# A fused convolution block on one Trainium2 core: the last group of its state stage in halves over three bank pairs, later weights on GpSimd, the triangle stage's input normalised group by group, convolutions issued in tap rows

## What is computed

```python
def _gn(v, G=32, eps=1e-05):
    m, s = mean and var over axes (1, 2, 4)
    return (g - m) / jnp.sqrt(s + eps)
x = x + L0(_gn(x))   # window attention
x = x + L1(_gn(x))   # state layer
x = x + L2(_gn(x))   # triangle product
x = x + L3(_gn(x))   # recurrence over 28 rows
```

```python
x1 = silu(depthwise_conv3x3(grouped_1x1(x, w1)))
u, z = in_proj(x1);  u = silu(conv1d_3taps(u) + conv1d_b)
dt, B, C = x_proj(u);  delta = softplus(dt @ dt_proj + b)
h = exp(delta * A) * h + (delta * u) * B      # scan over 784 pixels, per state n
y = sum over n of h_n * C_n;  y = (y + u * D_param) * silu(z)
x1 = out_proj(y);  x1 = (x1 - mu) * rsqrt(var + 1e-5) * gamma + beta
return grouped_1x1(x1 * silu(grouped_1x1(x, w2)), wout)
```

## Time and profile before

| | us |
|---|---|
| median of 3 runs | 523.81 |
| lowest, highest | 522.98, 526.88 |
| the profiled execution | 523.52 |
| its span, first to last instruction | 521.7 |
| mean granted TensorE clock | 0.862 of full |

### The profile page before, as it was taken

The page is one execution under the profiler, slowest core; times in us unless marked ns, Lnnn a source line. Parts: engine busy times, 40 slices in busy tenths (PEclk is TensorE's granted clock), DMA queues, the critical chain, the costliest instruction groups (busy, mean ns, idle before and its releaser), DMA issues.

```text
span 521.7 us, 10477 instructions
## 1 busy us (share of the span) xinstructions
PE 365.1 (70%) x3722; PEld 242.5 (46%) x3722; DVE 385.2 (74%) x687; ACT 304.9 (58%) x571; POOL 224.7 (43%) x201
## 2 busy tenths in 40 slices
PE   4189988887989788669857356144594354988885
PEld 3057666665755332323312112021574224977874
DVE  3897898898883698986999599995547595644444
ACT  4247888878775998893797424023865602434333
POOL 3626866774652519857869526750250000000000
PEclk9999999999899997986879667565796585999999
DMA  5110000000404031040000000000000000111111
GB/s 134 9 12 3 3 0 0 0 1 0 106 3 108 0 69 38 1 107 0 0 1 1 0 0 0 0 0 1 2 1 5 0 1 0 19 19 20 22 22 22
DMA packets 23879, 9.52 MB, mean 18 GB/s; under 512 B 20521, under 2 KB 22313, under 8 KB 23849
## 3 DMA queue, kind: packets, MB, share of 16 engines
q1 hardware_dynamic: 23720, 9.13, 8.8%
q0 software_dynamic: 128, 0.01, 0.1%
HBM read 2.00 MB, written 1.61 MB: 7 GB/s over the span
## 4 chain that ended last, share of the span: by engine, by line
DVE 29%; PE 26%; ACT 19%; issue 15%; SPq 5%; POOL 4%; DMA 1%; DVEq 1%; POOLq 0%; ACTq 0%
PE pair L1435 4%; DVE pair L1698 4%; DVE Hs L1705 3%; PE pair L993 3%; SPq L317 3%; PE pair L1130 3%; DVE Ts L1599 2%; PE pair L1198 2%; PE pair L1046 2%; ACT PT L647 2%; PE pair L1114 2%; POOL Pr L451 2%; DVE hC L1718 2%; ACT gates L943 2%; POOL pp L591 1%
## 5 line engine op out<-in xcount | busy, mean ns | idle before, releaser
L451 POOL TENSOR_TENSOR Pr<-Pr,rc 128x392 f32<-128x392 f32 x64 | 54.3, 880 | 41.3 <-DVE rc L1615 41.3
L485 POOL TENSOR_TENSOR YA<-YA,hC 128x784 f32<-128x784 f32 x28 | 52.8, 1886 | 38.0 <-DVE hC L1718 36.4
L1198 PE MATMUL pair<-BCf,sel 96*128 96x392 bf16 x128 | 38.5, 405 | 33.1 <-DVE Hs L1705 26.2
L1705 DVE TENSOR_TENSOR_SCAN Hs<-dA,pair 128x784 f32<-128x784 f32 x32 | 57.2, 1786 | 1.1
L1593 DVE TENSOR_REDUCE mx<-pair 128x8 f32<-128x392 f32 x64 | 32.9, 555 | 14.6 <-PE pair L993 14.6
L1198 PEld LDWEIGHTS pair<-BCf,sel 96*128 96x128 bf16 x128 | 10.7, 106 | 69.2 <-issue 67.0
L647 ACT ACTIVATE PT<-pair 128x512 f32<-128x512 f32 x64 | 37.7, 592 | 7.9 <-PE pair L1035 7.6
L1035 PE MATMUL pair<-ident,Pr 128*128 128x128 f32 x256 | 37.8, 287 | 2.4 <-ACT PT L647 1.2
L1718 DVE TENSOR_TENSOR hC<-Hs,pair 128x784 f32<-128x784 f32 x28 | 26.6, 950 | 14.5 <-PE pair L1198 14.5
L769 ACT ACTIVATE dA<-DL,Aneg 128x784 f32<-128x784 f32 x32 | 29.1, 941 | 13.5 <-DVE Hs L1705 13.4
L653 ACT ACTIVATE Pr<-Ts 128x392 f32<-128x392 f32 x64 | 34.5, 541 | 3.1 <-DVE Ts L1599 2.6
(11 more groups left out here) (216 smaller groups left out, 943.9 us busy)
## 6 DMA issues: line engine op xcount, KB each, us to landing
SX<-XP SPq DMA_DIRECT2D x48, 112.2 KB, 2.3
XT<-in_x SPq DMA_DIRECT2D x4, 392.0 KB, 5.4
out<-Os SPq DMA_DIRECT2D x28, 56.0 KB, 1.8
NB<-in_L_conv_x_proj_w SPq DMA_DIRECT2D x4, 3.0 KB
DW<-in_L_conv_dw SPq DMA_DIRECT2D x4, 1.1 KB
vec<-in_L_conv_b_qkv POOLq DMA_DIRECT2D x3, 0.5 KB, 6.0
W<-in_L_conv_w_qkv SPq DMA_DIRECT2D x1, 48.0 KB
BL<-in_L_conv_bi SPq DMA_DIRECT2D x3, 0.5 KB
```

Source lines behind the costliest of these rows:

```text
L451: eng.tensor_tensor(pg, pg, bcast(rc[:, g, :], 2, WT), ALU.mult).then_inc(pn_r, 1)
L485: eng.tensor_tensor(y, y, hC[:, n % NHC, :], ALU.add).then_inc(g_ya, 1)
L1198: ins = eng.matmul(SPREAD[s][:, HT * h:HT * h + HT], sel[:, n, :], upper(BCf[:, c % 2, s, HT * h:HT * h + HT]), start=True, stop=True)
L1705: eng.tensor_tensor_scan(Hs[:, n % 2, :], dA[:, n % NA, :], SPREAD[0], 0.0, ALU.mult, ALU.add).then_inc(v_s, 1)
```

## The change

- **Bank pairs.** `x2` of group 3 and `out`, `var` of group 2 move from pair 3 to pair 2. The last group's `out`, `var`, `wout` have pairs 2, 3 and 1 (`TAIL`), each bank with its own half.
- **Order in the slots.** `times_b(c+1, 0)` and its spread now come before the last `times_c` of group c. Convolutions are issued in pieces of one or two rows of taps between the spreads. In group 1 `out(0)`, `var(0)`, `gate(2)`, `x2(2)`, `inner(3, ·)` change places; in group 2 `x2(3)` comes before the spread of slot 7 and `gate(3)` behind all spreads. ScalarE's list in group 1 is reordered: `copy_bc(2, xC)` earlier, Ln and Exp paired, `decays(2, ·)` behind all the silus.
- **Gamma and beta.** Gamma goes into ScalarE's copy `cS`; beta and the gate become one VectorE instruction, `norm`, in place of `shift` on VectorE and `gated` on GpSimd.
- **Group 3.** VectorE also does `residual(1)`, `residual(2)`, the statistics of groups 0 and 1, and `norm(2)` between its slots, and `times_c(6)` before scan 7. GpSimd does `later_weights`, `later_biases`, the zeroing (only the pads of `XR`) and the skip term between its sums.
- **The tail**, for the last group, goes in halves of 392 columns. `spare` issues bf16 matmuls of 512 columns whose result nobody reads: 8, 6, 3, 3, 3, 4, 4 of them. ScalarE normalises groups 0 to 2 for the triangle stage itself (`Identity` with scale and bias) while the last group is still on its way; the last group's statistics go through Sqrt on ScalarE and a reciprocal on VectorE.
- **Memory.** `XR` becomes `XR0`, which lies over `SX`, and `XR1`.

```diff
+        TAIL = dict(out=2, var=3, wout=1)
+        def tail_result(name, h):
+            return pairs[TAIL[name]][:, h, 0:HT]
...
+        LAST_GROUP = {("x2", 3): 2, ("out", 2): 2, ("var", 2): 2}
...
+            def skip_term():
+                eng.wait_ge(a_ud, 1)
+                eng.wait_ge(v_c, DS * (J - 1) + 1)
+                y = YA[:, (J - 1) % 2, :]
+                eng.tensor_tensor(y, y, S1[:, 0, 0:T], ALU.add).then_inc(g_ud, 1)
+            def pads():
+                eng.wait_ge(p_["conv"], 2 * J)
+                eng.memset(XR0[:, :, :, W:32], 0.0).then_inc(t_zz, 1)
+                eng.wait_ge(v_dl, J)
+                eng.memset(XR1[:, :, :, H:32], 0.0).then_inc(t_zz, 1)
...
+            def later_weights():
+                loaded(eng, 2)
+                eng.tensor_scalar(vec[:, V_BO:V_BO + 1], vec[:, V_BO:V_BO + 1], 0.5, None, ALU.mult).then_inc(g_w, 1)
+                eng.tensor_scalar(W4[:, U_M:U_M + 4, :], W4[:, U_M:U_M + 4, :], 0.5, None, ALU.mult).then_inc(g_w, 1)
+                eng.wait_ge(g_w, 2)
+                eng.tensor_tensor(BD[:, U_A:U_Z, :].rearrange("p u (g c) -> p u g c", g=G), bcast(W4[:, U_A:U_Z, :], 2, G),
+                                  bcast(bcast(bd[:, :], 1, U_Z - U_A), 3, C), ALU.mult).then_inc(g_w, 1)
...
+                    pads()
+                    later_weights()
+                    skip_term()
+                    eng.wait_ge(g_ud, 1)
+                    add(3, 1)
+                    later_biases()
+                    add(3, 2)
+                    add(3, 3)
+                    scaled(2)
+                    eng.wait_ge(p_["z"], J)
+                    eng.wait_ge(p_["u"], 2 * J)
+                    eng.memset(Zc[:], 0.0).then_inc(t_zz, 1)
+                    add(3, 4)
+                    add(3, 5)
+                    add(3, 6)
...
                     decays(1, 5)
-                    sp_l(2)
                     out_m(0)
-                    sp_w(2)
                     copy_bc(2, 1, "xC")
                     decays(1, 6)
+                    sp_l(2)
+                    var_ln(0)
+                    sp_w(2)
+                    var_exp(0)
+                    decays(1, 7)
                     silu_conv(3, 0)
+                    silu_z(2)
                     silu_conv(3, 1)
-                    var_ln(0)
-                    decays(1, 7)
-                    var_exp(0)
...
+                    eng.activation(S1[:, 0, 0:T], US[:, J - 1, :], ACT.Identity, scale=vec[:, V_D:V_D + 1]).then_inc(a_ud, 1)
                     decays(3, 4, 5)
                     out_m(2)
-                    decays(3, 6, 7)
+                    decays(3, 6)
                     var_ln(2)
                     var_exp(2)
...
+            for h in range(2):
+                eng.wait_ge(p_["out"], J + h)
+                eng.activation(sq[:, columns(h)], tail_result("out", h), ACT.Square).then_inc(c_["out"], 1)
+                eng.activation(cS[:, columns(h)], tail_result("out", h), ACT.Identity, scale=vec[:, V_GA:V_GA + 1])
+            for h in range(2):
+                eng.wait_ge(p_["var"], J + h)
+                eng.activation(rs[:, columns(h)], tail_result("var", h), ACT.Ln, bias=epsc[:, 0:1]).then_inc(c_["var"], 1)
+            eng.wait_ge(n_mv, 4)
+            eng.activation(lnv[:, 0:J - 1], mv[:, 0:J - 1, 1], ACT.Ln, bias=epsc[:, 0:1]).then_inc(n_ln, 1)
+            for h in range(2):
+                eng.wait_ge(c_["var"], J + h)
+                eng.activation(rs[:, columns(h)], rs[:, columns(h)], ACT.Exp, scale=-0.5).then_inc(a_rs, 1)
+            eng.wait_ge(n_ln, 1)
+            eng.activation(rstd[:, 0:J - 1], lnv[:, 0:J - 1], ACT.Exp, scale=-0.5).then_inc(n_rs, 1)
+            eng.wait_ge(n_nm, 1)
+            for j in range(J - 1):
+                eng.activation(XR0[:, :, j, 0:W], X[:, T * j:T * j + T].rearrange("p (y x) -> p y x", y=H), ACT.Identity,
+                               scale=rstd[:, j:j + 1], bias=nmr[:, j:j + 1]).then_inc(n_x0, 1)
+            eng.wait_ge(n_mv, 5)
+            eng.activation(lnv[:, J - 1:J], mv[:, J - 1:J, 1], ACT.Sqrt, bias=epsc[:, 0:1]).then_inc(n_sd, 1)
             for j in range(J):
...
+            def spare(n, bk):
+                for _ in range(n):
+                    eng.matmul(banks[bk][:, :], sel[:, 0, :], sel[:, 0:4, :].rearrange("p n c -> p (n c)"), start=True, stop=True)
...
+                    bc("B", 4)
+                    conv(2, 0, (0, 1))
+                    bc("C", 3)
+                    bc("B", 5)
+                    conv(2, 0, (2,))
+                    conv(2, 1, (0,))
+                    bc("C", 4)
+                    bc("B", 6)
+                    conv(2, 1, (1, 2))
+                    bc("C", 5)
...
+                    out(0)
+                    bc("B", 3)
+                    bc("C", 2)
+                    var(0)
+                    bc("B", 4)
+                    conv(3, 0, (0, 1))
+                    bc("C", 3)
+                    bc("B", 5)
+                    conv(3, 0, (2,))
+                    bc("C", 4)
+                    gate(2)
+                    bc("B", 6)
+                    conv(3, 1, (0, 1))
+                    bc("C", 5)
+                    conv(3, 1, (2,))
+                    x2(2)
+                    bc("B", 7)
                     inner(3, 0)
-                    spread("B", 6)
+                    bc("C", 6)
...
+                    x2(3)
+                    bc("B", 7)
+                    bc("C", 6)
+                    spread(3, "B", 0)
+                    bc("C", 7)
                     gate(3)
...
+                    wout(1)
+                    bc("C", 1)
+                    out(2)
+                    bc("B", 3)
+                    bc("C", 2)
+                    bc("B", 4)
+                    var(2)
+                    bc("C", 3)
+                    bc("B", 5)
+                    bc("C", 4)
+                    bc("B", 6)
+                    bc("C", 5)
+                    wout(2)
+                    bc("B", 7)
+                    bc("C", 6)
+                    bc("C", 7)
+            eng.wait_ge(s1z, 1)
...
+            eng.wait_ge(v_s, DS * J)
+            spare(8, 0)
+            eng.wait_ge(c_["var"], J - 1)
+            for h in range(2):
+                eng.wait_ge(v_y2, J + h)
+                eng.matmul(tail_result("out", h), BD[:, U_OUT, :], yz[:, columns(h)], start=True, stop=True).then_inc(p_["out"], 1)
+            eng.wait_ge(c_["wout"], J - 1)
+            for h in range(2):
+                eng.wait_ge(c_["out"], J + h)
+                eng.matmul(tail_result("var", h), VB[:, :], sq[:, columns(h)], start=True, stop=True).then_inc(p_["var"], 1)
+            spare(6, 0)
+            eng.wait_ge(v_c7, 2)
+            for h in range(2):
+                eng.wait_ge(c_["var"], J + h)
+                spare(3, 0)
+            eng.wait_ge(a_rs, J)
+            spare(3, 0)
+            for h in range(2):
+                eng.wait_ge(v_nt, J + h)
+                eng.matmul(tail_result("wout", h), BD[:, U_WO, :], nt[:, columns(h)], start=True, stop=True).then_inc(p_["wout"], 1)
+            for h in range(2):
+                eng.wait_ge(c_["wout"], J + h)
+                spare(4, 0)
...
+            def norm(w):
+                eng.wait_ge(g_nt0, w + 1)
+                eng.wait_ge(c_["x2"], w + 1)
+                eng.scalar_tensor_tensor(nt[:, :], nt[:, :], vec[:, V_BE:V_BE + 1], X2[:, w, :], ALU.add, ALU.mult).then_inc(v_nt, 1)
...
+                if c < J - 1:
+                    slot(c, 7)
+                    times_c(c, 6)
+                    if c == 0:
+                        delta_u(1)
+                    times_b(c + 1, 0)
+                    times_c(c, 7)
...
+            c = J - 1
+            eng.wait_ge(p_["C"], DS * J)
+            eng.wait_ge(v_s, DS * J)
+            ring_free(c, DS - 1)
+            for h in range(2):
+                eng.tensor_tensor(hC[:, (DS - 1) % NHC, columns(h)], Hs[:, (DS - 1) % 2, columns(h)], SPREAD[1][:, columns(h)], ALU.mult).then_inc(v_c7, 1)
+            eng.wait_ge(g_ya, (DS - 1) * c + DS - 2)
+            eng.wait_ge(p_["out"], J - 1)
+            eng.wait_ge(c_["z"], J)
+            for h in range(2):
+                yh = yz[:, columns(h)]
+                eng.wait_ge(v_c7, h + 1)
+                eng.tensor_tensor(yh, YA[:, c % 2, columns(h)], hC[:, (DS - 1) % NHC, columns(h)], ALU.add).then_inc(v_y1, 1)
+                eng.wait_ge(v_y1, J + h)
+                eng.tensor_tensor(yh, yh, ZS[:, J - 1, columns(h)], ALU.mult).then_inc(v_y2, 1)
+            eng.wait_ge(c_["wout"], J - 1)
+            link(column_stats(2))
+            for j in range(J - 1):
+                ins = eng.bn_aggr(mv[:, j, :], stats[:, j].rearrange("p h s -> p (h s)"))
+            ins.then_inc(n_mv, 1)
+            eng.wait_ge(p_["wout"], J - 1)
+            eng.wait_ge(c_["x2"], J)
+            for h in range(2):
+                nh = nt[:, columns(h)]
+                eng.wait_ge(a_rs, J + h)
```

(33 more changed lines are left out.)

637 lines of the change are left out of this document (259 added, 378 removed).

## The result

| | before | changed | ratio (95% interval) |
|---|---|---|---|
| median of the runs | 523.4 us (4 runs, 522.98 to 526.88) | 501.5 us (4 runs, 498.30 to 502.39) | 0.9581 (0.9543 to 0.9619) |
| profiled execution | 523.5, span 521.7 | 501.33, span 499.3 | |

Forecast: 505, between 495 and 513. The experiments need marks that can be found in every trace: the first scan of each group, E (the end of the last scan of group 3), the first triangle matmul, and the end.

The account below looks back on a forecast made before the run. No engine fills the span: VectorE waits for TensorE in groups 1 and 2, VectorE bounds group 3, and the tail is one chain handed round. 523.5 - 0.3 - 2.5 - 5.7 + 9.0 - 19.1 = 504.9, forecast 505 us, range 495 to 513.

Parts of the forecast that it names:

- three signs of being wrong: A later_weights GpSimd instruction over 7 us, scan 7 waiting for a sum, or last-half wout starting after 17.5 us of tail.
- Groups 0 and 1: First two groups of the state stage: gain 0.3 (0 to 1.5) in group 0, 2.5 (0 to 5.5) in group 1.
- the open point: TensorE's clock in group 1: gain 5.5 at 2.4 GHz, nothing at 1.2 GHz; taken as back after the last tap, 2.5.
- the 2 us at slot 7: Group 1, slot 6 to 7: TensorE's work takes 5.6 us at the 1.2 GHz level against 3.6.
- Group 2: Third group: gain 5.7 (5 to 6); the 5.98 us wait behind x2(3) goes, norm for shift costs 0.3.
- Group 3: Last group, bound by VectorE: cost 9.0 (6.1 to 13), from 6.2 added instructions, 2.2 GpSimd collisions and 0.6 late spread.
- The third term: Group 3: var(2) at 2.98 us between two spreads makes one spread late by about 0.6 us.
- The tail: Last scan to first triangle matmul: 20.4 us instead of 40.2, net gain 19.1 (16 to 21.5).
- The 0.7 given back: Triangle stage start: TensorE's second gate product waits for ScalarE's transposing copies, ending 4.8 us after the first matmul, against 3.9.
- The spares: Tail: they let var and wout run at the higher clock, saving 1.5 us already covered by ScalarE's loads, so nothing.

Follow-up runs that it names:

- the second execution: The changed kernel measured once more, unedited: 499.88 us, ratio 0.9541 to the kernel before.
- `x2(3)` alone: Kernel before, with only x2(3) moved to pair 2 instead of pair 3: 518.97 us, ratio 0.9883.
- the weights: Kernel before, with only later_weights and later_biases moved to GpSimd in group 3: 522.17 us, ratio 0.9977.
- the early normalisation: Changed kernel with ScalarE's normalisations of groups 0 to 2 made to wait for group 3's statistics: 503.88 us, ratio 0.9597.
- the tail whole: Changed kernel with out, var, norm, wout and residual of group 3 in one piece each instead of halves: 499.66 us, ratio 0.9529.
- the Newton tail: Changed kernel with VectorE computing the reciprocal roots by three Newton steps and normalising groups 0 to 2 instead of ScalarE: 498.00 us, ratio 0.9465.
- all edits: Changed kernel with skip term held until outputs(2), VectorE's Newton roots and normalisation, outputs(0) late and remainder(2) held: 495.15 us, ratio 0.9466.
- skip term late: Changed kernel with GpSimd's skip term held until outputs(2) is done: 497.15 us, ratio 0.9506.
- the held remainder: Changed kernel with outputs(0) behind group 1's first slot and GpSimd's remainder(2) held until outputs(0) is done: 501.30 us, ratio 0.9564.

## Why the prediction was right, point by point

The forecast difference was -18.6, that of the two spans is -22.4. Of the 3.8 between them, 2.1 are group 3, 1.5 the tail, 0.4 the stretch ahead and 0.3 the one behind; groups 0 to 2 came out 0.5 the other way (-8.0 for -8.5; -8.6 in the second execution). None of the three signs of being wrong appeared: the longest GpSimd instruction of `later_weights` took 2.54 us, scan 7 waited for no sum, and `wout` of the last half began 14.0 us after E.

- **Groups 0 and 1.** -3.7 and -2.4 us in two executions of the same code, forecast -2.8. The -1.9 of group 0 in the first is the clock's, for the two kernels that keep the old order there had 33.47 and 33.45. Compared at the same clock in group 0, the two groups together gained 3.9 to 4.2 (73.07 for 77.00 and 77.27) or 2.4 (74.35 for 76.77). The clock in group 1 was the open point, and it was placed wrongly. The prediction held it at 0.50 through the taps; it was 0.52 and 0.50 from 225 to 235, under `out(0)` and `var(0)`, and 0.95 from 235 to 240, where two rows of taps took 1.61 us for the 2.4 counted. So the 2 us at slot 7 never came. VectorE waited for TensorE 0.47 and 1.10 before the products of slots 3 and 4, and 0.91 at the first product of group 2, which was foreseen. That GpSimd is next was missing: the prediction let group 1 wait for TensorE alone (1.74 for GpSimd before `outputs(0)`, or 1.67 before DU in the second execution). The size came near, but partly by luck.
- **Group 2.** -4.3 and -6.2, forecast -5.7. The wait of 5.98 went, and `x2(3)` alone showed -4.2. Of the 1.8 between the two executions 1.1 is DU beside GpSimd (2.69 in the one, 1.56 in the other, 1.90 before) and 0.5 a wait for TensorE that only the first has. The prediction left DU's collision as it was, and it moves with GpSimd's queue.
- **Group 3.** The term was sized too high: +6.9 for 9.0. The added instructions, start to start, took 5.9 (norm twice for one `shift` 1.40, residuals 1.76, statistics 1.89, `times_c(6)` 0.88), forecast 6.2 (its parts add up to 6.3). Collisions took 1.5, all of it the one product beside the skip term, forecast 2.2. The third term, 0.6 for a late spread, did not appear: VectorE's wait for TensorE is 0.47 in both kernels, and its idle time in the group fell from 1.1 to 0.8. The parts exceed the 6.9 by 0.6, of which that is 0.3; the other 0.3 isn't placed. The 1408-column weights took 2.54 us, within the 1.63 to 6.8 given and below the 3.4 taken.
- **The tail.** -20.6 for -19.1, of which 19.8 was the shift of the first product. The order and the releasers came out as written: second Exp half at 11.9 us from E (13.3), Identities at 16.9 (17.5), Sqrt 18.6 (19.1), first product 19.6 (20.4). A spare took 0.45 for 0.48 and ScalarE's Square of a half 0.50 for 0.585; VectorE's two steps and `nmr` took 2.1 from the second Exp to the end of `nmr`, where 1.3 was counted. Of the 20.6 the runs isolate 2.75 for the weights, 2.3 to 2.5 for the early normalisation and 0.6 to 0.8 for the halves. The largest link, 10.2 from `out` to `var`, is read from the two timelines; which share of it is `wout(2)` with its residual, the statistics or the new bank pairs no run shows.
- **The 0.7 given back** did not appear: the third gate product comes 8.3 us after the first triangle product, 8.5 before. The prediction let ScalarE's copies set it in both kernels. Before, TensorE's own first 32 products took 5.56 us; after, with a granted clock of 0.57 from 348 to 352, they take 5.29, and copies that end 4.5 us behind the first product are still covered. That the copies are next the runs show: with the tail whole the 32 products took 3.81 at full clock, TensorE then waited 1.48 for ScalarE's gate, and the third gate product came after 8.4 all the same. With the Newton tail, also 3.81, and two of the copies done early, it came after 6.7. The 32 products in the changed kernel and with the tail whole:

```profile
348.43 5.29 PE L1425 MATMUL pair<-BD,SX 128*128 128x128 f32 x32 [2.98 <-DVE SX L1909]
```

```profile
346.97 3.81 PE L1424 MATMUL pair<-BD,SX 128*128 128x128 f32 x32 [1.08 <-DVE SX L1903]
```

- **The spares.** The prediction gave them nothing, and in the changed kernel they are worth nothing measurable. Whether they help where the tail is shorter, as in the Newton tail, was not tried.

The collisions follow the Trainium skill, "SBUF — State Buffer", "Who interferes with whom": a VectorE instruction with two SBUF inputs waits for a GpSimd instruction that reads SBUF. The trace agrees: `yz` ended 0.83 us behind the skip term (302.11 and 301.28), and again 0.83 behind the 1408-column product (304.79 and 303.96), each time nearly its own length (0.97) after the other's end. GpSimd's instruction, which began first, is longer too: 2.50 for 1.84, 3.31 for 2.54. The prediction took the W4 scaling of 6.73 us for the same thing. But that instruction (`TENSOR_SCALAR W<-W`) has one input, and what stood beside it was a memset, which reads nothing; no run here tests that pair.

## What to carry to other kernels

When the profile shows a long instruction in a tail, ask what stands behind it in the same queue: taken away alone, the weights gave 2.75 us of tail and no measurable time; in the changed kernel, with the previous group's `wout` and residual moved out as well, `var` followed `out` after 2.4 us instead of 12.6. Work that goes to another engine has to be placed against the bound engine's two-input instructions too; one wait that kept a GpSimd sum from a VectorE product gave 1.5 us. And compare stretches between marks, over more than one execution of the same code, before an edit gets the credit: 2 us of group 0 came and went with the granted clock, and so did the wait for GpSimd behind it.

## What the runs showed of the hardware that had not been expected

- The granted clock in one stretch of one code differs between executions: 1.00 in one and 0.57 in the other from 198 to 207 us (one convolution piece 1.52 and 2.84 us). Over fourteen profiles it is 1.00 or 0.50 from 200 to 207, seven of each.
- Between an Ln and the Exp that follows it stands a table load of 1.28 us, in the tail (338.42) and in the triangle stage (L984 at 389.01), and the load costs just that, as the prediction had counted: ScalarE's Ln of the small rows ended at 338.40 and Exp started at 339.72. The Trainium skill, "ScalarE: Activation LUTs", "Table sets: the hidden batching unit", has one set for both and so one load; the trace has two, and the measurement decides.
- Spares up to 345.45 did not keep the clock for the products that start at 348.43: TensorE had idled 2.98 us, and 32 of them took 5.29 us (granted clock 0.57 from 348 to 352). With 1.08 to 1.54 us idle behind the spares the same 32 took 3.81 at 1.00 in four profiles (tail whole, Newton, all edits, skip term late). With 1.78 idle they took 5.44 in one (the held remainder), so the gap alone doesn't decide it.
